# A fused stencil and pooled-attention kernel: ScalarE's early work reordered, and one product of two late pairs moved from VectorE to GpSimd

## What is computed

```python
def _L0_cond_ref(y, zX, zY, zR, dx, dy):          # reflected edges
    lap_x = (yp_x[:, :, :-2] - 2.0 * y + yp_x[:, :, 2:])
    lap_y = (yp_y[:, :-2, :] - 2.0 * y + yp_y[:, 2:, :])
    return zX * lap_x + zY * lap_y + zR * y * (1.0 - y)

def _L1_cond_ref(hidden, W1, b1, v, prompt_type_ids):
    attn_in = tanh(einsum('bsd,da->bsa', hidden, W1) + b1)
    scores = einsum('bsa,a->bs', attn_in, v)
    # the mask is a prefix, a suffix or all but the diagonal
    p = softmax(where(mask, scores[:, None, :], -1e30))
    return einsum('bjl,bld->bjd', p, hidden) / cnt[..., None]

x = x + _L0_cond_ref(x, ...)        # the result is called x1
x = x + _L1_cond_ref(x, ...)
```

## Time and profile before

| | |
|---|---|
| median of 3 runs | 107.56 us (107.21 to 107.77) |
| profiled execution | 107.45 us |
| its span in the trace | 105.7 us |
| busy PE, DVE, ACT, POOL | 98.6, 86.2, 82.4, 65.7 us |
| granted clock of TensorE | 0.995 |

### The profile page before, as it was taken

The page is one execution under the profiler, slowest core; times in us unless marked ns, Lnnn a source line. Parts: engine busy times, 40 slices in busy tenths (PEclk is TensorE's granted clock), DMA queues, the critical chain, the costliest instruction groups (busy, mean ns, idle before and its releaser), DMA issues. The chain is left out here.

```text
span 105.7 us, 1690 instructions
## 1 busy us (share of the span) xinstructions
PE 98.6 (93%) x416; PEld 57.2 (54%) x416; DVE 86.2 (82%) x118; ACT 82.4 (78%) x212; POOL 65.7 (62%) x64
## 2 busy tenths in 40 slices
PE   6999999989999999999999999998999899999920
PEld 3534586963674468456645574565456644655600
DVE  4289988999697878999999999999999994326960
ACT  0499977899988889988897699997978883689500
POOL 5579959699999997989598959695900100010000
PEclk9999999999999999999999999999999999999997
DMA  0999999999999999999999999860506052305873
GB/s 12 297 276 354 384 415 414 416 429 409 416 418 371 381 265 397 407 420 370 398 379 389 389 377 415 334 244 5 195 0 202 0 195 79 122 31 171 267 249 119
DMA packets 10199, 30.16 MB, mean 285 GB/s; under 512 B 740, under 2 KB 1286, under 8 KB 10188
## 3 DMA queue, kind: packets, MB, share of 16 engines
q1 hardware_dynamic: 10060, 29.96, 76.1%
q10 hardware_dynamic: 128, 0.09, 0.3%
HBM read 21.66 MB, written 8.39 MB: 284 GB/s over the span
## 5 line engine op out<-in xcount | busy, mean ns | idle before, releaser
L731 POOL TENSOR_TENSOR sq<-xin 128x1024 f32<-128x1024 f32 (+1 forms) x13 | 29.7, 2281 | 1.1 <-DMA xin<-in_x 1.1
L1215 PE MATMUL U<-X,M 128*128 128x512 f32 x60 | 30.2, 609 | 0.0
L1145 PE MATMUL hps<-x1T,W1s 128*128 128x512 f32 (+1 forms) x72 | 29.1, 547 | 0.0
L715 POOL TENSOR_TENSOR lr<-xin 128x1020 f32<-128x1020 f32 (+1 forms) x15 | 27.4, 1831 | 2.7 <-DMA xin<-in_x 2.7
L937 DVE SCALAR_TENSOR_TENSOR outs<-U,fac,X 128x512 f32<-128x512 f32 x30 | 21.5, 747 | 4.1 <-ACT X L515 3.0
L1145 PEld LDWEIGHTS hps<-x1T,W1s 128*128 128x128 f32 x72 | 13.2, 190 | 13.5 <-issue 10.8
L1132 PE MATMUL tps<-ident,X 128*128 128x128 f32 x132 | 18.1, 278 | 1.0 <-DVE X L884 0.8
L446 ACT ACTIVATE x1T<-tps 128x512 f32<-128x512 f32 x33 | 17.7, 587 | 1.5 <-PE tps L1132 1.4
L515 ACT ACTIVATE X<-U 1x512 f32<-1x512 f32 x29 | 16.5, 580 | 2.4 <-PE U L1215 1.8
L770 POOL TENSOR_TENSOR cs<-cs,e 128x2 f32<-128x2 f32 x16 | 3.1, 194 | 21.7 <-ACT e L466 20.6
L884 DVE SCALAR_TENSOR_TENSOR X<-lr,z,xps 128x1024 f32<-128x1024 f32 (+1 forms) x13 | 16.1, 1239 | 0.4
(11 more groups left out here) (124 smaller groups left out, 91.8 us busy)
## 6 DMA issues: line engine op xcount, KB each, us to landing
xin<-in_x SPq DMA_DIRECT2D x11, 1536.0 KB, 9.8
out<-outs SPq DMA_DIRECT2D x14, 504.0 KB
xin<-in_x SPq DMA_DIRECT2D x5, 512.0 KB, 7.5
out<-outs SPq DMA_DIRECT2D x4, 252.0 KB
xin<-in_x SPq DMA_DIRECT2D x2, 256.0 KB, 3.8
xin<-in_x SPq DMA_DIRECT2D x2, 252.0 KB
xin<-in_x SPq DMA_DIRECT2D x4, 66.0 KB
W1s<-in_L_cond_W SPq DMA_DIRECT2D x1, 256.0 KB, 7.3
```

The lines of the kernel that those rows point to most:

```text
L715: pool.tensor_tensor(to[:, :, 1:D - 1], src[:, :, 0:D - 2], src[:, :, 2:D], ALU.add).then_inc(s_lr, 1)
L731: pool.tensor_tensor(sq[:, p % 3, 0:w, :], x3[:, p % XS, 0:w, 0, :], x3[:, p % XS, 0:w, 2, :], ALU.add).then_inc(s_ud, 1)
L1145: last = mm(hps[:, part], W1s[:, c, :], x1T[:, k % 2, c, part], start=(c == 0), stop=(c == DC - 1))
L1215: mm(bank(j), M4[:, k % 2, i - GB * k, :], X1[:, i, :], start=True, stop=True).then_inc(s_U, 1)
```

## The change

It has three parts, and computes the same.

1. **Pairs 13 and 15** (`THERE`). Their home is their own place in `X1`, in SBUF. ACT writes the factor there, POOL multiplies it by x there (`multiplied_there`), and DVE has two instructions left for the pair (`evict_there`, then the last of `evict`), both with both tensors in SBUF. ACT makes these factors earlier in the round, in front of two carries. The factors of pairs 14 and 16 no longer wait for pairs 13 and 15 to be evicted.
2. **ACT's early order.** The factor of pair 3 stands in front of two `keep_x1T`, and the factor of pair 5 behind `tanh(0)` instead of in front of it.
3. **The masks of the last tile** (`masks_last`, four instructions) go from the start to round 6.

```diff
+THERE = (13, 15)
...
         def home(p):
+            if p in THERE:
+                return X1[:, 2 * p:2 * p + 2, :]
             return U if p in (1, 3, 5) else xps
+        def multiplied(p):
+            return aside(p) - sum(q <= p for q in THERE)
         def gone(p):
-            return {1: 0, 2: 1, 3: 2, 4: 3, 5: 4, 6: 5}.get(p, p)
+            return {1: 0, 2: 1, 3: 2, 4: 3, 5: 4, 6: 5, 13: 11, 14: 13, 15: 13, 16: 15}.get(p, p)
...
             masks()
+            factor_of_x(3)
             for i in (2, 3):
                 keep_x1T(i)
-            factor_of_x(3)
...
             biases()
+            tanh(0)
             factor_of_x(5)
-            tanh(0)
...
                     for i in group(k + 1)[2:4]:
                         keep_x1T(i)
+                    if 2 * k + 5 in THERE:
+                        factor_of_x(2 * k + 5)
                     carry(j + 2)
                     carry(j + 3)
                     if k == 4:
                         halves_taken()
+                    if k == KG - 2:
+                        masks_last()
                     if k > 1:
                         weights(k)
-                    if 2 * k + 5 < PAIRS:
+                    if 2 * k + 5 < PAIRS and 2 * k + 5 not in THERE:
                         factor_of_x(2 * k + 5)
...
+            def multiplied_there(p):
+                pool.wait_ge(s_u, aside(p))
+                pool.tensor_tensor(home(p), home(p), xin[:, p % XS, :, :], ALU.mult).then_inc(s_there, 1)
...
                 sums(k)
-                if 2 * k + 6 < PAIRS:
+                if k == KG - 4:
+                    left_right(2 * k + 6)
+                    multiplied_there(2 * k + 5)
+                    above_below(2 * k + 6)
+                elif k == KG - 3:
+                    multiplied_there(2 * k + 5)
+                    local(2 * k + 6)
+                elif 2 * k + 6 < PAIRS:
                     local(2 * k + 6)
...
+            def evict_there(p):
+                n, to = kind(p), home(p)
+                dve.wait_ge(s_there, THERE.index(p) + 1)
+                dve.wait_ge(s_ud, aside(p))
+                vec.scalar_tensor_tensor(out=to, in0=sq[:, p % 3, :, :], scalar=z[:, 1, n:n + 1], in1=to,
                                          op0=ALU.mult, op1=ALU.add).then_inc(s_vert, 1)
```

More of the change, by code:

```diff
@@ L176, in build @@
         s_ux = sem("s_ux")
+        s_there = sem("s_factors_times_x_in_x1")
         s_ud = sem("s_ud")
@@ L300, in load @@
                     if q in ASIDE:
-                        sp.wait_ge(s_ux, aside(q))
+                        sp.wait_ge(s_ux, multiplied(q))
                         sp.wait_ge(s_ud, aside(q))
@@ L535, in masks, with masks_last @@
                 act.wait_ge(s_sel, 1)
+                nc.scalar.activation(maskT[:, 0, 0:1], scl[:, 0:1], ACT.Copy).then_inc(s_mk, 1)
+                act.wait_ge(s_mk, 1)
+                nc.scalar.activation(maskT[0:1, 0, 0:1], one[0:1, 0:1], ACT.Copy).then_inc(s_msk, 1)
+            def masks_last():
                 other = maskT[0:HALF, 1, HALF:P]
                 nc.scalar.activation(other, other, ACT.Copy, scale=0.0).then_inc(s_mk, 1)
-                act.wait_ge(s_mk, 1)
+                act.wait_ge(s_mk, 2)
                 nc.scalar.activation(triC[:, :], maskT[:, 1, :], ACT.Copy).then_inc(s_mk, 1)
-                act.wait_ge(s_mk, 2)
+                act.wait_ge(s_mk, 3)
                 for to in (triC[0:1, 1:P], triC[HALF:HALF + 1, HALF + 1:P]):
                     nc.scalar.activation(to, to, ACT.Copy, scale=0.0).then_inc(s_mk, 1)
-                nc.scalar.activation(maskT[:, 0, 0:1], scl[:, 0:1], ACT.Copy).then_inc(s_mk, 1)
-                act.wait_ge(s_mk, 5)
-                nc.scalar.activation(maskT[0:1, 0, 0:1], one[0:1, 0:1], ACT.Copy).then_inc(s_msk, 1)
             def counts():
@@ L861, in evict_begin @@
                 vec.tensor_tensor(to, to, xin[:, p % XS, 0:w, :], ALU.mult).then_inc(s_ux, 1)
-                m = aside(p)
-                dve.wait_ge(s_ux, m)
-                dve.wait_ge(s_ud, m)
+                dve.wait_ge(s_ux, multiplied(p))
+                dve.wait_ge(s_ud, aside(p))
                 vec.scalar_tensor_tensor(out=to, in0=sq[:, p % 3, 0:w, :], scalar=z[:, 1, n:n + 1], in1=to,
+                                         op0=ALU.mult, op1=ALU.add).then_inc(s_vert, 1)
+            def evict_there(p):
+                n, to = kind(p), home(p)
+                dve.wait_ge(s_there, THERE.index(p) + 1)
+                dve.wait_ge(s_ud, aside(p))
+                vec.scalar_tensor_tensor(out=to, in0=sq[:, p % 3, :, :], scalar=z[:, 1, n:n + 1], in1=to,
                                          op0=ALU.mult, op1=ALU.add).then_inc(s_vert, 1)
@@ L871, in evict @@
                     m = aside(p)
-                    if not begun:
+                    if p in THERE:
+                        evict_there(p)
+                    elif not begun:
                         evict_begin(p)
@@ L1194, in lengths_last @@
                 to = sps[:, LC + LAST:LC + TILES]
+                pe.wait_ge(s_mk, 5)
                 pe.wait_ge(s_cs, 2 * KG + 1)
```

## The result

The changed kernel takes 112.71 us (median of 4 runs, 111.84 to 113.94), beside 107.41 us for the kernel before (107.21 to 107.77) on the same chip. The ratio is 1.046, with a 95% interval of 1.038 to 1.055. The forecast was slower, at 110.2 us and at most 110.8. Ratios here leave out executions that are more than 1.5% above the fastest of their kernel, and medians do not.

The account below looks back on a forecast made before the run. PE was taken to set the end, waiting for DVE late in the kernel. 107.45 + 2.2 (pairs 13 and 15) + 0.55 (tanh) = 110.2 us, masks 0; own range 109.4 to 110.8, whole range 106.3 to 110.8.

Parts of the forecast that it names:

- What bounds the kernel: Whole kernel: PE sets the end, waiting for DVE late; an earlier DVE could give back at most 1.41 us.
- The product on POOL: Pair 13's product on POOL: 2.37 us, ending at 67.61, before DVE's two outputs end at 67.86.
- The exclusion: Pairs 13 and 15: DVE steps with two SBUF inputs and POOL's reads block each other for whole instructions; forecast's chance 0.42.
- Pair 13 "comes 2.50 us later": Pair 13 on DVE: taking turns with POOL, its last step ends at 74.44 instead of 71.94.
- "PE's transposes, which waited for it already, move with it": PE at pair 13: its transposes shift by the same 2.50 us as DVE's last step.
- Pair 15, "+2.21 us": Transposes of pair 15: PE's queue, free at 84.78 instead of 82.57, sets them 2.21 us later, rounded to 2.2.
- The tanh, "+0.55 us": Early part: ACT's tanh must wait for W1 of group 0, so W1 of group 1 comes 0.55 us later.
- The masks: Round 6 on ACT: four instructions of 1.2 us, covered by 1.68 us of idle time, so 0.
- POOL keeps the port: Rival: at pair 13 DVE gets in only after POOL's queued work, 5.4 us late; 113.4 us, chance 0.10.

Follow-up runs that it names:

- e12: Kernel before with only pair 13's product on POOL, POOL waiting for that pair's eviction, ACT's order and masks as before: 106.35 us, ratio 0.988.
- e10: Changed kernel with ACT's order and masks as before, plus three products of ones on PE ahead of pair 13's transposes: 108.99 us, ratio 1.012.
- e4: Changed kernel plus three products of ones on PE in the gap ahead of pair 13's transposes: 109.83 us, ratio 1.023.
- e8: Kernel before with one more DVE product, one input in PSUM and one in SBUF, ahead of pair 13's last step: 109.48 us, ratio 1.019.
- e9: Kernel before with two more DVE products, one input in PSUM and one in SBUF, ahead of pair 13's last step: 110.48 us, ratio 1.031.
- e11: Kernel before with ACT's new order, moved masks and one product of ones on PE ahead of W1 of group 1: 108.10 us, ratio 1.006.
- e1: Kernel before with only ACT's new order and the masks moved to round 6: 109.69 us, ratio 1.019.
- e3: Changed kernel with POOL waiting for the evictions of pairs 13 and 15, reading nothing during DVE's two steps: 110.94 us.
- e13: Same as e12 but without POOL's wait for pair 13's eviction: 109.86 us, ratio 1.026.
- e5: Kernel before with one edit, tanh of group 0 ahead of the factor of pair 5: 108.74 us, ratio 1.010.
- e7: Changed kernel with POOL waiting for the evictions of pairs 13 and 15, ACT's order and masks as before: 107.73 us, ratio 1.001.

## Why the prediction was right in its direction and wrong in its size

- **What bounds the kernel**: right. PE waited for DVE at pairs 13 and 15 and was the bound elsewhere. e12 gave back 1.0 us of the 1.41 at most that the rows allowed.
- **The product on POOL**: right. It takes 2.36 us (forecast 2.37) and ended 0.18 us before DVE asked for it. This cover is thin: in e10 a late load used it up.
- **The exclusion**, read from one row of 0.50 us: right, and so was the order of the turns, on thin evidence, as the forecast said. The changed kernel's own set-up confirms the reading of that row. There POOL's L725 was over at 5.00, before DVE came, and the same step takes 0.36:

```profile
5.24 0.36 DVE L864 SCALAR_TENSOR_TENSOR U<-ident,off 128x128 f32<-128x128 f32 x1
```

```profile
3.97 1.03 POOL L725 TENSOR_TENSOR lr<-xin 128x510 f32<-128x510 f32 x1 [0.44 <-DMA xin<-in_x]
```

- **Pair 13 "comes 2.50 us later"**: too large by 0.60. It is 1.90 behind what the early shift explains. A held step ends 1.08 us after the other engine's instruction, and POOL's `lr` 1.75, where the forecast took 1.29 and 1.89.
- **"PE's transposes, which waited for it already, move with it"**: this is the step that failed. PE does not only move. It stood idle for 2.38 us, and the work behind the gap ran at 1.2 GHz: +2.36 us to W1 of group 6 and +0.40 in it, 2.76 us together. The forecast named the gap ("PE sits idle about 3 us") as a sign to look for, and gave it no price of its own. e4 measures this term alone at 2.9 us by filling the gap, and e8 and e9 make such a fall with no exclusion. With the other terms as measured and no fall, the sum would have been 107.45 + 0.78 + 1.31 = 109.5 us; the clock is what takes it to 112.3.
- **Pair 15, "+2.21 us"**: the number came from PE's own queue, moved by pair 13, and this is how it went. PE was later still, so DVE's steps of 1.43 and 2.17 us were hidden. But PE got back 0.60 us there, where the forecast subtracted the 0.29 of the bracket in the earlier trace rows. So beside its clock the exclusion costs 1.3 us (1.91 - 0.60) and not 2.2, and e10 measures 1.3 in its undelayed executions.
- **The tanh, "+0.55 us"**: the mechanism and the size were right, with 0.62 us in the rows and 0.7 in e11. Missing again was the clock. The gap of 1.14 us that the order opens is followed by the half clock in part of the executions, at 1.7 us in the traces of e1 and e3. The changed kernel's profiled execution was spared there.
- **The masks**, priced at nothing: right. They take 1.19 us in round 6, and ACT is still idle for 0.44 us in front of the next tanh.
- **The rivals**: "POOL keeps the port" gave 113.4 us and came nearest to 112.7, but not for its reason. POOL gave way after each instruction.

**What stays open**: why the same gap is followed by the half clock in one execution and not in another, and why it costs 1.2 us behind one gap of 2.4 us (e13) and 2.8 behind another (the changed kernel). In the traces the half clock follows gaps of 1.14 to 2.74 us. It does not follow the gaps of 1.14 us in those of the changed kernel, e4 and e5, nor those of 1.0 us in e3 and e7, nor any of 0.2 to 0.64 us within the stream. The mean clock of an execution tells a fall only roughly: the traces of e4, e7 and e10 have 0.986 and 0.987 with no fall behind a gap.

## What to carry to other kernels

When work moves from DVE to GpSimd and its data moves to SBUF with it, look at the inputs of the DVE instructions that are left. Two inputs in SBUF beside a reading GpSimd take turns with it, instruction by instruction, and a wait that holds GpSimd back for the two steps can be worth more than the work that was moved. And price a new gap on TensorE twice: once for its length, and once for the half clock that may follow. Here the second was larger than the first (2.76 and 1.91 us).

## What the runs showed of the hardware

- DVE and POOL exclude each other for a whole instruction, in the order of asking: DVE steps of 1.28 us took 3.23 and 2.79, and POOL's of 1.89 and 2.37 took 2.88 and 3.33. Back-to-back work of POOL did not shut DVE out.
- A held DVE step ended 1.08 us after the other engine's instruction, 0.2 less than its 1.28, at both steps of pair 13 and, within 0.01, again at both of pair 15. What passes in these 0.2 us is not shown.
- A gap of only 1.14 us on PE was followed by the half clock in some executions, which made W1 of a group 1.7 us longer (e1, e3); with one product of ones in the gap none of ten executions shows it (e11).
